# Mean layers: extra columns summed in a zeroed room of their own, among the additions of gathered quads, and added to the sums in seven wide parts

## The chip, the cores and the metric

The kernel runs on one core of a Trainium2 chip. The metric is the device time of one execution in microseconds (us), as the median of a few runs. Engines are named as in the profile: PE (TensorE matmul; PEld is its weight load), DVE (VectorE), ACT (ScalarE), POOL (GpSimd), SP (SyncE, which here issues transfers). "L2227" is line 2227 of the kernel before.

## The reference, cut to what matters

The program is a chain of four graph networks on 6250 nodes of 128 features and 106250 edges sorted by destination. The change lies in the third of them, three mean ("SAGE") layers in a row, and in the residual sum after them:

```python
deg = segment_sum(ones(src.shape[0]), dst, num_segments=n)
inv_deg = (1.0 / maximum(deg, 1.0))[:, None]
def sage_conv(h, Wl, b, Wr):
    agg = segment_sum(h[src], dst, num_segments=n) * inv_deg
    return agg @ Wl + b + h @ Wr
h = relu(sage_conv(x, W_l0, b0, W_r0))
h = relu(sage_conv(h, W_l1, b1, W_r1))
x = layernorm(x + sage_conv(h, W_l2, b2, W_r2))
```

## The kernel before, in words

Nodes lie in 49 blocks of 128 (`BLOCKS`), edges in 832 tiles of 128 (`TILES`). The sum over edges, `agg` (features on partitions, one column for each node), is made in two ways at once in each mean layer.

**Gathered tiles.** 288 tiles (`RUN`) are gathered. POOL issues one indirect DMA for a tile (L2140, `pool_rows`), 16 slots of `G` deep: before the first tile of quad q it waits until PE has used quad q-4. ACT makes one-hot matrices (L2148). PE multiplies a quad of four tiles into one of three banks (L2162, `pe_sum_quad`; 8 matmul records for each quad) and must find the additions of quad q-3 done. DVE adds each of the four 128x128 results to a window of `agg` whose start is read from a table (L2227): 72 quads, q = 0 to 71.

**Dense part.** All other edges are in an adjacency matrix in DRAM, which SP loads (L2102, L2107, `sp_adjacency`, four slots) and PE multiplies with three bf16 planes of the node rows (L2126, `pe_dense`) in 115 steps. Steps 0 to 16 give 544 "extra" columns (`extra`, one for each dense tile: what falls to the tile's first node). Steps 17 to 65 and 66 to 114 give the sums of two halves of the other nodes. `keep_extras` (L2210) copies the extras out of the banks, `add_half` (L2202) adds a half, five windows of 418 columns, to `agg`; PE waits for each (`adj_read`) before it uses the banks again. PE's order is written out by hand: behind step n come the quads `quads_by(n)` to `quads_by(n + 1)`, so that quads 0 to 3 come before step 17, about two quads follow three steps from there on, quads 36 and 37 come before step 66, and quad 71 comes last.

**Extras.** DVE adds each extra column to `agg` at a start read from the table: 8 after the additions of every quad from quad 4 (`EARLY_QUADS`) to quad 71 (`add_extras`, L2193). Each waits for the one before it.

After quad 71 come `add_half(1)` and one last addition of 418 columns (L2236). Then the next block of the program begins: PE multiplies `agg` with the weights (L2026). In the third mean layer, DVE also adds the residual, `hT += xT` over all 6272 columns (L2233), after quad 40; SP has loaded `xT` from DRAM (L2335) between the adjacency steps 40 and 41.

Of the kernel before, what the change touches and what calls it, by code (L numbers as in the profile page):

```python
# [15 lines left out]
P = 128  # L16
NODES = 6250
EDGES = 106250
D = 128
# [119 lines left out]
def build_program(nc, a, out):  # L139
    with ExitStack() as ctx:  # L140
# [130 lines left out]
        c_extra = signal("extra_added")  # L271
        residual_in = signal("residual_in")
        runs_ready = signal("runs_ready")
# [1891 lines left out]
        EXTRAS_A_QUAD = 8  # L2165
        EARLY_QUADS = quads_by(FIRST_STEPS)
        assert (RUN_QUADS - EARLY_QUADS) * EXTRAS_A_QUAD >= DENSE
        EXTRA_ADDS = DENSE + 2 * NODE_BANKS

        def dve_sums(l):  # L2170


            n = [0, 0]

            def after_adds():
                dve.wait_ge(c_added.sem, c_added.at(n[0]))

            def after_extra():
                if n[1]:
                    dve.wait_ge(c_extra.sem, c_extra.at(n[1]))  # L2180

            extras_left = [DENSE]
# [12 lines left out]

            def add_half(half):
                after_adds()
                dve.wait_ge(adj_used.sem, adj_used.at(FIRST_STEPS + (half + 1) * BLOCKS))
                for c in range(NODE_BANKS):
                    w = agg[:, bass.ds(chunk_start(DVE, half * NODE_BANKS + c), BANK_COLS)]  # L2200
                    after_extra()
                    dve.tensor_tensor(w, w, bank[c][:, 0:BANK_COLS], ALU.add).then_inc(c_extra.sem, 1)  # L2202
                    n[1] += 1
                after_extra()
                dve.sem_inc(adj_read.sem, 1)
# [7 lines left out]

            half_quads = quads_by(FIRST_STEPS + BLOCKS) - 2
            for q in range(RUN_QUADS):
                if q == EARLY_QUADS:
                    keep_extras()
                if q == half_quads:
                    add_half(0)
                windows = window_at(DVE, DENSE + q * QUAD, QUAD)  # L2220
                dve.wait_ge(c_rows.sem, c_rows.at(q + 1))
                after_extra()
                for k in range(QUAD):
                    if n[0]:
                        after_adds()
# [8 lines left out]
            add_half(1)  # L2234

            dve.tensor_tensor(agg[:, 0:BANK_COLS], agg[:, 0:BANK_COLS], agg[:, NODES:], ALU.add)  # L2236

        def sums_passed():
# [4 lines left out]
            for c, n in ((c_rows, RUN_QUADS), (c_onehot, RUN_QUADS), (c_far, RUN_QUADS), (c_added, RUN), (c_extra, EXTRA_ADDS), (adj_used, STEPS), (adj_read, 3),  # L2243
# [83 lines left out]
        for l in range(1, 3):  # L2327
            with nc.Block() as block:
                @block.sync
                def _(_e):  # L2330
                    sp_sage_weights(l)
                    sp_adjacency(0, FIRST_STEPS + BLOCKS // 2)
                    if l == 2:
                        sp.wait_ge(own_rows.sem, own_rows.at(GROUPS))
# [53 lines left out]
            if l == 2:  # L2388
                residual_in.passed(16)
# [387 lines left out]
```

## Time and profile before

| | |
|---|---|
| median of 3 runs | 7239.66 us (7233.92 to 7249.64) |
| the profiled execution's own time | 7241.22 us |
| its span | 7239.4 us |
| the three mean layers, from the first gather to the first matmul behind the last | about 4737 to 6028 us |
| busy share of the span | PE 76%, DVE 65%, ACT 31%, POOL 69% |

The rows below come from that execution. In a row of the timeline the first number is the start (us from the span's start), the second the length, then engine, line, operation, the tiles out<-in, the shape, and how many instructions were merged; in brackets is the idle time of the engine before them and what ended it.

### The profile page before, as it was taken

Reading aid. Unit: us, or ns where it says so; the run is one execution under the profiler, and the core shown is the slowest. Engines: PE = TensorE matmul, PEld = TensorE weight load, DVE = VectorE, ACT = ScalarE, POOL = GpSimd, SP = SyncE. Lnnn points to the kernel's source line nnn. Section 1 sums busy time; section 2 is a strip of 40 time slices with the busy share of each in tenths; the row PEclk is TensorE's granted clock in tenths of the full one; section 3 lists DMA queues with packets and bytes.
Section 4 is the critical chain, followed back from the end, with each engine's and each line's share of the span. In section 5 each row is a group of like instructions: output and inputs, shape, how many; then the busy total and the mean of one; then the engine's idle time right before and its main releaser. Section 6 shows DMA issues by size and latency. Waiting matters only on the chain. (4 is left out here: it accounts for less than half of the span.)

```text
span 7239.4 us, 119762 instructions
## 1 busy us (share of the span) xinstructions
PE 5528.3 (76%) x30345; PEld 4159.5 (57%) x30345; DVE 4732.1 (65%) x20294; ACT 2265.0 (31%) x5973; POOL 4967.1 (69%) x5179
## 2 busy tenths in 40 slices
PE   4675667777777767777767777789898996888887
PEld 3442344556656556656656566666665665666665
DVE  7985678466666456666546666664545556888887
ACT  1044443211114311113411112543333333454554
POOL 5777764677777577777577777657475673777774
PEclk7688888788888778888878888899999997998898
DMA  9433352577777467777567777667576762222222
GB/s 306 133 79 87 78 114 51 164 207 208 207 211 220 140 193 209 209 210 221 159 179 208 208 205 209 185 185 208 159 207 179 209 205 73 56 57 56 56 57 53
DMA packets 911701, 1151.31 MB, mean 159 GB/s; under 512 B 143234, under 2 KB 676290, under 8 KB 911106
## 3 DMA queue, kind: packets, MB, share of 16 engines
q1 hardware_dynamic: 689296, 673.54, 30.7%
q0 software_dynamic: 202464, 461.07, 23.8%
q10 hardware_dynamic: 19346, 9.66, 0.5%
q8 instruction: 265, 4.34, 0.2%
q14 instruction: 330, 2.70, 0.1%
HBM read 882.09 MB, written 261.74 MB: 158 GB/s over the span
## 5 line engine op out<-in xcount | busy, mean ns | idle before, releaser
L498 POOL DMA_INDIRECT G<-table_kv,idx x2496 | 2381.6, 954 | 956.0 <-issue 744.6
L1708 DVE SCALAR_TENSOR_TENSOR sums<-ramp,place,bank 128x128 f32<-128x128 f32 x2496 | 718.6, 343 | 1180.1 <-PE bank L1627 1084.3
L1617 PE MATMUL bank<-ident,G 128*128 128x128 f32 x2496 | 649.2, 337 | 708.0 <-DMA G<-table_kv,idx 701.1
L2140 POOL DMA_INDIRECT G<-table_h,src_idx x864 | 823.0, 953 | 480.5 <-issue 256.6
L1596 ACT COPY slab<-bank 128x512 f32<-128x512 f32 x624 | 364.0, 583 | 2293.4 <-PE bank L1617 2293.2
L498 POOL DMA_INDIRECT G<-table_h,idx x832 | 828.9, 996 | 301.4 <-issue 228.2
L1627 PE MATMUL bank<-qT,slab 128*128 x4992 | 906.9, 339 | 99.6 <-issue 82.2
L1617 PEld LDWEIGHTS bank<-ident,G 128*128 128x128 f32 x2496 | 382.7, 164 | 928.1 <-DMA G<-table_kv,idx 885.5
L1627 PEld LDWEIGHTS bank<-qT,slab 128*128 128x128 f32 x4992 | 793.9, 242 | 197.8 <-issue 196.8
L1839 DVE TENSOR_SCALAR OH<-ramp,place,weight 128x128 f32<-128x128 f32 x2076 | 721.7, 357 | 13.8 <-issue 6.9
L2126 PE MATMUL bank<-sums,qT 128*128 128x418 bf16 (+1 forms) x3528 | 672.2, 333 | 33.4 <-DVE same L2049 12.3
L1671 PE MATMUL bank<-OH,sums 128*128 128x128 f32 x3648 | 627.0, 327 | 24.2 <-DVE sums L1848 16.0
L898 POOL DMA_INDIRECT adjacency<-sums x544 | 526.9, 969 | 171.2 <-issue 165.2
L2602 PEld LDWEIGHTS bank<-OH,qT 128*128 128x128 f32 x3328 | 466.6, 223 | 283.0 <-DVE qT L2667 246.0
L2602 PE MATMUL bank<-OH,qT 128*128 128x128 f32 x3328 | 494.8, 311 | 127.2 <-DVE sums L2680 125.8
L1671 PEld LDWEIGHTS bank<-OH,sums 128*128 128x128 f32 x3648 | 564.0, 236 | 46.5 <-DVE sums L1848 28.3
L1848 DVE TENSOR_TENSOR sums<-sums,bank 128x128 f32 x1824 | 506.5, 278 | 3.6 <-issue 2.7
L2193 DVE TENSOR_TENSOR sums<-sums,rows 128x1 f32 x1632 | 267.0, 164 | 346.9 <-DVE sums L2227 108.3
L2126 PEld LDWEIGHTS bank<-sums,qT 128*128 128x128 bf16 x3528 | 346.0, 98 | 256.8 <-issue 36.2
L2148 ACT ACTIVATE OH<-ramp,place 128x128 f32<-128x128 f32 x864 | 275.9, 390 | 673.9 <-PE bank L2162 666.0
L2227 DVE TENSOR_TENSOR sums<-sums,bank 128x128 f32 x864 | 249.7, 289 | 213.3 <-DVE sums L2193 83.5
L2680 DVE TENSOR_TENSOR sums<-sums,bank 128x256 f32 x832 | 347.2, 417 | 62.3 <-issue 59.4
(351 smaller groups left out, 9582.8 us busy)
## 6 DMA issues: line engine op xcount, KB each, us to landing
stash<-G SPq DMA_DIRECT2D x312, 512.0 KB
sums<-stash SPq DMA_DIRECT2D x624, 256.0 KB
sums<-adjacency SPq DMA_DIRECT2D x294, 522.5 KB
adjacency<-same SPq DMA_DIRECT2D x49, 1184.0 KB
same<-adjacency SPq DMA_DIRECT2D x90, 522.5 KB
G<-table_kv,idx POOLq DMA_INDIRECT x2496
sums<-adjacency SPq DMA_DIRECT2D x48, 408.0 KB
table_kv<-G SPq DMA_DIRECT2D x72, 256.0 KB, 3.3
```

Of the source, the lines that this page charges most:

```text
L498: pool.indirect_dma_start(G[:, s, 0:width], None, tab, bass.IndirectOffsetOnAxis(ap=idx[:, s:s + 1], axis=0)).then_inc(c_gather[s].sem, 16)
L898: pool.indirect_dma_start(adj_cells, bass.IndirectOffsetOnAxis(ap=cell[:, d:d + 1], axis=0), count[:, d:d + 1], None).then_inc(scattered[i ...
L1596: act.copy(quad(KT, q).rearrange("p s d -> p (s d)"), bank[q % 2][:, :]).then_inc(c_kt.sem, 1)
L1617: ins = pe.transpose(bank[q % 2][:, (s % QUAD) * P:(s % QUAD + 1) * P], G[:, s, 0:D], ident[:])
L1627: ins = pe.matmul(bank[2 + q % 2][:, (s % QUAD) * P:(s % QUAD + 1) * P], KT[:, s, :], w, start=True, stop=True)
L1671: ins = pe.matmul(into[:, k * P:(k + 1) * P], v_rows[:, s, :], OH[:, s, :], start=True, stop=True)
L1708: ins = dve.scalar_tensor_tensor(scratch[:, s, :], ramp[:], place[:, n * QUAD + s:n * QUAD + s + 1], bank[2 + q % 2][:, s * P:(s + 1) * P] ...
L1839: ins = dve.tensor_scalar(OH[:, s, :], ramp[:], place[:, t:t + 1], weight[:, t:t + 1], ALU.is_equal, ALU.mult)
L1848: dve.tensor_tensor(w, w, bank[SUM_BANKS[q_add % 2]][:, k * P:(k + 1) * P], ALU.add).then_inc(c_added.sem, 1)
L2126: ins = pe.matmul(bank[c][:, 0:width], plane[k][:, b * P:(b + 1) * P], adj_slot[s][:, j * at + c * width:j * at + (c + 1) * width], start= ...
L2140: pool.indirect_dma_start(G[:, s, 0:D], None, table[l], bass.IndirectOffsetOnAxis(ap=src_idx[:, DENSE + t:DENSE + t + 1], axis=0)).then_in ...
L2602: ins = pe.matmul(o, msg[:, s, part * D:(part + 1) * D], OH[:, s, :], start=True, stop=True)
```

## The change

Four things. The `xT` space, which holds nothing that is needed in this stage, is zeroed in seven parts before quad 0. The extra columns are added there, at their node's column, and no longer to `agg`: 10 in a quad, in the quads 4 to 58, two or three ahead of each of the quad's four additions. After the quads 59 to 65, one part of 896 columns of `xT` is added to `agg`. And since `xT` is taken, the residual of the third layer goes through other spaces in four pieces (16, 16, 1 and 16 blocks): three are loaded before adjacency step 17, the fourth before step 41 once the first has been added, and they are added to `hT` after the quads 12, 16, 17 and 34. Each chain of additions waits for its own predecessor: an extra for the extra before it, an addition to `agg` for the addition to `agg` before it.

```diff
-        EXTRAS_A_QUAD = 8
+        EXTRAS_A_QUAD = 10
         EARLY_QUADS = quads_by(FIRST_STEPS)
+        EXTRA_QUADS = -(-DENSE // EXTRAS_A_QUAD)
+        PLACED_QUAD = EARLY_QUADS + EXTRA_QUADS
+        PLACED_PARTS = 7
+        PLACED = NP // PLACED_PARTS
+        RESIDUAL_QUADS = (EARLY_QUADS + 8, EARLY_QUADS + 12, EARLY_QUADS + 13, EARLY_QUADS + 30)
+        FIRST_RESIDUALS = 3
...
-            def add_extras(k):
-                after_adds()
-                done = DENSE - extras_left[0]
-                extras_left[0] -= k
-                for d in range(done, done + k, QUAD):
-                    windows = window_at(DVE, d, QUAD)
-                    for j in range(QUAD):
-                        after_extra()
-                        w = agg[:, bass.ds(windows[j], 1)]
-                        dve.tensor_tensor(w, w, extra[:, d + j:d + j + 1], ALU.add).then_inc(c_extra.sem, 1)
-                        n[1] += 1
...
+            def place_extra(d, node):
+
+                dve.wait_ge(c_extra.sem, c_extra.at(X_PARTS + d))
+                w = xT[:, bass.ds(node, 1)]
+                dve.tensor_tensor(w, w, extra[:, d:d + 1], ALU.add).then_inc(c_extra.sem, 1)
+
+            for part in range(X_PARTS):
+                dve.memset(xT[:, part * PLACED:(part + 1) * PLACED], 0.0).then_inc(c_extra.sem, 1)
             half_quads = quads_by(FIRST_STEPS + BLOCKS) - 2
             for q in range(RUN_QUADS):
                 if q == EARLY_QUADS:
                     keep_extras()
                 if q == half_quads:
                     add_half(0)
+                done = max(0, q - EARLY_QUADS) * EXTRAS_A_QUAD
+                extras = range(done, min(DENSE, done + EXTRAS_A_QUAD) if q >= EARLY_QUADS else done)
                 windows = window_at(DVE, DENSE + q * QUAD, QUAD)
-                dve.wait_ge(c_rows.sem, c_rows.at(q + 1))
-                after_extra()
+                places = dict(zip(extras, window_at(DVE, done, len(extras)) if extras else ()))
                 for k in range(QUAD):
-                    if n[0]:
-                        after_adds()
+                    for d in extras[len(extras) * k // QUAD:len(extras) * (k + 1) // QUAD]:
+                        place_extra(d, places[d])
+                    if k == 0:
+                        dve.wait_ge(c_rows.sem, c_rows.at(q + 1))
+                    after_last()
                     w = agg[:, bass.ds(windows[k], P)]
                     dve.tensor_tensor(w, w, bank[SUM_BANKS[q % 3]][:, k * P:(k + 1) * P], ALU.add).then_inc(c_added.sem, 1)
-                    n[0] += 1
-                if q >= EARLY_QUADS and extras_left[0]:
-                    add_extras(min(EXTRAS_A_QUAD, extras_left[0]))
-                if l == 2 and q == half_quads + 4:
-                    dve.wait_ge(residual_in.sem, residual_in.at(16))
-                    dve.tensor_tensor(hT[:], hT[:], xT[:], ALU.add)
+                    next_is(c_added, q * QUAD + k + 1)
+                part = q - PLACED_QUAD
+                if part in range(PLACED_PARTS):
+                    if part == 0:
+                        dve.wait_ge(c_extra.sem, c_extra.at(X_PARTS + DENSE))
+                    at = slice(part * PLACED, (part + 1) * PLACED)
+                    add_whole(agg[:, at], xT[:, at])
+                if l == 2 and q in RESIDUAL_QUADS:
+                    r = RESIDUAL_QUADS.index(q)
+                    dve.wait_ge(residual_in.sem, residual_in.at(16 * max(r + 1, FIRST_RESIDUALS)))
+                    home, b0, nb = residual_rows(r)
+                    dve.tensor_tensor(nodes_h[:, b0:b0 + nb, :], nodes_h[:, b0:b0 + nb, :], home, ALU.add).then_inc(residual_added.sem, 1)
             add_half(1)
...
+        def residual_rows(r):
+
+            b0 = (0, SLAB_BLOCKS, BLOCKS - 1, 2 * SLAB_BLOCKS)[r]
+            slab_rows = slab[:, 0:SLAB_BLOCKS * D].rearrange("p (b d) -> p b d", d=D)
+            home = (slab_rows, G[:, :, D:2 * D], dst_part[:, 0:D].unsqueeze(1), slab_rows)[r]
+            return home, b0, home.shape[1]
...
                     sp_sage_weights(l)
-                    sp_adjacency(0, FIRST_STEPS + BLOCKS // 2)
+                    sp_adjacency(0, FIRST_STEPS)
                     if l == 2:
-                        sp.wait_ge(own_rows.sem, own_rows.at(GROUPS))
-                        sp.dma_start(xT[:].rearrange("p (b d) -> p b d", d=D), table[0].rearrange("(b p) d -> p b d", p=P)).then_inc(residual_in.sem, 16)
+                        for r in range(FIRST_RESIDUALS):
+                            sp_residual(r)
+                    sp_adjacency(FIRST_STEPS, FIRST_STEPS + BLOCKS // 2)
+                    if l == 2:
+                        sp.wait_ge(residual_added.sem, residual_added.at(1))
+                        sp_residual(FIRST_RESIDUALS)
                     sp_adjacency(FIRST_STEPS + BLOCKS // 2, STEPS)
```

## Rows read from the trace of the kernel before

**Rows 1.** Waits by engine pair, PE only, 5149 to 5588 and 5588 to 6028.

```profile
PE bank L2026 <- PEq L2251: 22.1, 1, 22.1
PE bank L2026 <- PEq L2328: 21.5, 1, 21.5
...
PE bank L2026 <- PEq L2328: 21.8, 1, 21.8
PE bank L2126 <- DMA sums<-adjacency: 4.2, 1, 4.2
```

**Rows 2.** Timeline of PE and DVE, end of layer one; last row: layer two.

```profile
5126.06 1.13 PE L2162 MATMUL bank<-OH,G 128*128 128x128 f32 x8
...
5139.57 1.55 DVE L2227 TENSOR_TENSOR sums<-sums,bank 128x128 f32 x4 [0.45 <-DVE sums L2193]
5141.65 1.03 DVE L2193 TENSOR_TENSOR sums<-sums,rows 128x1 f32 x4 [0.53 <-DVE sums L2227]
5143.03 1.03 DVE L2193 TENSOR_TENSOR sums<-sums,rows 128x1 f32 x4 [0.35 <-DVE sums L2193]
5144.48 3.48 DVE L2202 TENSOR_TENSOR sums<-sums,bank 128x418 f32 x5 [0.41 <-DVE sums L2193]
5148.10 0.60 DVE L2236 TENSOR_TENSOR sums<-sums 128x418 f32<-128x418 f32 x1
...
5560.88 1.13 PE L2162 MATMUL bank<-OH,G 128*128 128x128 f32 x8 [0.42 <-issue]
```

**Rows 3.** Gathers L2140 by stretch: us, POOL busy (count), PEclk, DMA share, GB/s.

```profile
4785.40:5124.80 339.40, 256.66 (x272) 0.99 0.70 208
5219.30:5558.70 339.40, 256.65 (x272) 0.99 0.70 208
5652.90:5998.20 345.30, 262.63 (x272) 0.99 0.72 214
```

**Rows 4.** By stretch: us; PE, PEld, DVE, ACT, POOL busy; PEclk, DMA share, GB/s.

```profile
4963.30:5127.20 163.90, 163.81 (x1007) 104.81 (x1007) 80.41 (x391) 57.22 (x150) 122.13 (x130) 0.99 0.69 200
5835.60:6006.00 170.40, 165.66 (x1007) 103.73 (x1007) 86.87 (x392) 57.22 (x150) 124.46 (x126) 0.99 0.65 191
...
5646.00:5656.00 10.00, 10.00 (x90) 9.30 (x90) 4.86 (x12) 3.23 (x10) 2.46 (x3) 1.00 0.28 81
```

**Rows 5.** Timeline: POOL gathers beside DVE additions of two SBUF operands.

```profile
5860.84 6.69 DVE L2233 TENSOR_TENSOR hT<-hT,xT 128x6272 f32<-128x6272 f32 x1
5861.40 6.95 POOL L2140 DMA_INDIRECT G<-table_h,src_idx  x1 [0.31 <-issue]
...
5170.70 0.68 DVE L2046 TENSOR_TENSOR sums<-hT,qT 128x512 f32<-128x512 f32 x1
5171.17 1.02 POOL L2140 DMA_INDIRECT G<-table_h,src_idx  x1 [0.30 <-issue]
5171.30 0.69 DVE L2047 TENSOR_TENSOR qT<-hT,qT 128x512 bf16<-128x512 f32 x1
```

**Rows 6.** Timeline: DVE in quads 0 to 3, PE at step 17.

```profile
5215.91 0.89 DVE L2081 TENSOR_TENSOR hT<-bank,bias_rows 128x512 f32<-128x512 f32 x2 [0.20 <-PE bank L2072]
5219.23 1.55 DVE L2227 TENSOR_TENSOR sums<-sums,bank 128x128 f32 x4 [2.43 <-PE bank L2162]
5221.08 1.55 DVE L2227 TENSOR_TENSOR sums<-sums,bank 128x128 f32 x4 [0.30 <-DVE sums L2227]
5226.12 1.55 DVE L2227 TENSOR_TENSOR sums<-sums,bank 128x128 f32 x4 [1.45 <-PE bank L2162]
...
4794.64 1.94 PE L2126 MATMUL bank<-sums,qT 128*128 128x418 bf16 x10 [1.83 <-DVE rows L2210]
5662.08 1.94 PE L2126 MATMUL bank<-sums,qT 128*128 128x418 bf16 x10 [1.83 <-DVE rows L2210]
```

**Rows 7.** A memset of DVE: ns minimum/median/maximum.

```profile
L1948 DVE MEMSET rows<- x3: 698/698/698, 1320.3 to 3592.1; 128x768 f32 x3
```

**Rows 8.** The residual's transfer L2335, from issue to landing (minimum, median, maximum).

```profile
DMA to landing us min/median/max: 18.1/18.1/18.1
```

More of the change, by code:

```diff
@@ L271, in build_program @@
         c_extra = signal("extra_added")
+        c_whole = signal("whole_parts_added")
         residual_in = signal("residual_in")
+        residual_added = signal("residual_added")
         runs_ready = signal("runs_ready")
@@ new lines, in build_program, with after_last, next_is, add_whole @@
+        PLACED_QUAD = EARLY_QUADS + EXTRA_QUADS
+        PLACED_PARTS = 7
+        PLACED = NP // PLACED_PARTS
+        assert PLACED_QUAD + PLACED_PARTS <= RUN_QUADS and PLACED * PLACED_PARTS == NP
+        RESIDUAL_QUADS = (EARLY_QUADS + 8, EARLY_QUADS + 12, EARLY_QUADS + 13, EARLY_QUADS + 30)
+        FIRST_RESIDUALS = 3
+        WHOLE_ADDS = PLACED_PARTS + 2 * NODE_BANKS
+        def dve_sums(l):
+            last = []
+            def after_last():
+                for sem, n in last:
+                    dve.wait_ge(sem, n)
+            def next_is(c, n):
+                last[:] = [(c.sem, c.at(n))]
+            wholes = [0]
+            def add_whole(w, part):
+                after_last()
+                dve.tensor_tensor(w, w, part, ALU.add).then_inc(c_whole.sem, 1)
+                wholes[0] += 1
+                next_is(c_whole, wholes[0])
@@ L2196, in add_half @@
             def add_half(half):
-                after_adds()
                 dve.wait_ge(adj_used.sem, adj_used.at(FIRST_STEPS + (half + 1) * BLOCKS))
                 for c in range(NODE_BANKS):
-                    w = agg[:, bass.ds(chunk_start(DVE, half * NODE_BANKS + c), BANK_COLS)]
-                    after_extra()
-                    dve.tensor_tensor(w, w, bank[c][:, 0:BANK_COLS], ALU.add).then_inc(c_extra.sem, 1)
-                    n[1] += 1
-                after_extra()
+                    add_whole(agg[:, bass.ds(chunk_start(DVE, half * NODE_BANKS + c), BANK_COLS)], bank[c][:, 0:BANK_COLS])
@@ L2205, in add_half @@
+                after_last()
                 dve.sem_inc(adj_read.sem, 1)
@@ L2238, in sums_passed, with sp_residual @@
+        assert SLAB_BLOCKS == SLOTS and 3 * SLAB_BLOCKS + 1 == BLOCKS
+        def sp_residual(r):
+            home, b0, nb = residual_rows(r)
+            sp.dma_start(home, table[0][b0 * P:(b0 + nb) * P, :].rearrange("(b p) d -> p b d", p=P)).then_inc(residual_in.sem, 16)
         def sums_passed():
@@ L2242, in sums_passed @@
                 c.passed(16 * len(range(k, STEPS, ADJ_SLOTS)))
-            for c, n in ((c_rows, RUN_QUADS), (c_onehot, RUN_QUADS), (c_far, RUN_QUADS), (c_added, RUN), (c_extra, EXTRA_ADDS), (adj_used, STEPS), (adj_read, 3),
+            for c, n in ((c_rows, RUN_QUADS), (c_onehot, RUN_QUADS), (c_far, RUN_QUADS), (c_added, RUN), (c_extra, X_PARTS + DENSE), (c_whole, WHOLE_ADDS), (adj_used, STEPS), (adj_read, 3),
                          (turned_rows, GROUPS), (turned_kept, GROUPS), (own_rows, GROUPS), (own_kept, GROUPS), (planes_ready, GROUPS), (residual_done, GROUPS),
@@ L2388, in build_program @@
             if l == 2:
-                residual_in.passed(16)
+                residual_in.passed(16 * (FIRST_RESIDUALS + 1))
+                residual_added.passed(FIRST_RESIDUALS + 1)
         wup = wts[:, 0:D]
```

14 lines of the change are left out of this document (3 added, 11 removed).

## The prediction

> **What bounds the kernel now.** I read the waits of PE over the mean layers first. PE's longest waits are three of 21.5 to 22.1 us, one behind each mean layer [rows 1]. The timeline shows what PE waits for: its last quad ends at 5127.19, and DVE goes on to 5148.70, adding quads 69 to 71, their extras, the second half and the last 418 columns, before the next block starts at 5149.30 [rows 2, 1]. DVE is some 2.5 quads behind by then, because one of its quads with 8 extras takes about 4.95 us (0.45 + 1.55 + 0.53 + 1.03 + 0.35 + 1.03) [rows 2], against 163.9/34 = 4.82 us of PE (34 quads and 49 steps in the second half) [rows 4].
>
> Before that tail it is not DVE that sets the pace. POOL's 272 gathers of quads 4 to 71 take 339.4 us in the first two layers, 1.248 us each and without a pause [rows 3], that is 4.99 us for a quad, and PE's last quad ends 2.4 us after the last gather is issued (5124.8, 5127.19) [rows 3, 2]. So in the first layer POOL's chain and PE's end together; in the second PE ends at 5562.0, 3.3 us after POOL [rows 2, 3], which leaves POOL about 0.9 us of slack. In the third POOL takes 345.3 us [rows 3] and PE's second half 170.4 us instead of 163.9 [rows 4]: DVE's residual addition of 6.69 us holds up a gather (6.95 us instead of 0.94) [rows 5] and puts DVE so far behind that PE must wait for banks.
>
> **The change part by part.**
>
> *Extras leave the tail.* They end with quad 58, the parts with quad 65, so quads 66 to 71 are additions only: 1.85 us from one to the next (5219.23, 5221.08) [rows 6], and DVE will wait for PE. The new gap of PE behind a layer is 0.14 (a quad's end to its first addition, my estimate from waits between engines) + 1.55 + 0.41 + 3.48 + 0.14 + 0.60 + 0.60 to the next block = 6.9 us [rows 2]. Against 22.1, 21.5 and 21.8 [rows 1] this saves 15.2 + 14.6 + 14.9 = **44.7 us**. It holds whenever DVE is caught up by quad 71.
>
> *A quad with ten extras.* Chained extras follow at (1.03 - 0.16)/3 = 0.29 us [rows 2]. The trace does not show one between additions. Where an operation waits for nothing recent, it can start about when the one before ends: L2047 starts at 5171.30, before L2046's recorded end at 5171.38 [rows 5]. So I count 6 chained steps x 0.29, 4 from extra to addition x 0.16, 3 from addition to extra x 0.29, and the last addition with two table loads behind it, 0.29 + about 0.7 (one load leaves 0.30 to 0.45 idle [rows 6, 2]): 4.2 us. Upper bound: each of the 14 at its chained pitch, 4 x 0.42 + 10 x 0.29 + 0.7 = 5.3 us. I take 4.2, as nothing recent is waited for. Below 4.82 it costs nothing: PE's matmuls cover it.
>
> *Seven wide parts.* From 418 columns in 0.60 and 6272 in 6.69 us [rows 2, 5] a column costs 1.04 ns, so 896 take 1.09 us. With two chained waits a quad takes 3.1 us, under PE's 4.82, so nothing on DVE. But both operands lie in SBUF, as with L2233, and then a gather that starts during the addition is held until it ends: the gather of 5861.40 ended 0.86 after L2233, that of 5171.17 was 0.08 longer because L2046 ran until 5171.38 [rows 5]. With a gather every 1.248 us an addition of length L under that costs POOL L²/(2 x 1.248) on average, 0.48 us for a part, **3.3 us** a layer (bounds: 0, and 7 x 1.09 = 7.6). The Trainium skill, "SBUF — State Buffer", section "Who interferes with whom", says that a DVE instruction with two SBUF inputs contends with a GpSimd instruction that reads SBUF, but infers that `tensor_tensor` leaves descriptor generation alone; by the inference the 3.3 would be 0. The 6.95 us gather [rows 5] speaks against the inference, and that case is a rival below.
>
> *The residual in four pieces.* 16 blocks are 2048 columns, 6.69 - 4224 x 0.00104 = 2.29 us. Longer than the gathers' period, each costs POOL 2.29 - 0.62 = 1.67, three of them 5.0 us (bounds 0 and 6.9), against the 6.0 (6.95 - 0.94) of before. On DVE they come one at a time, while there is time to spare.
>
> *The memsets.* 0.698 us for 768 columns [rows 7] make 0.81 for 896, 5.7 in all. In the second layer DVE is free from 5216.80, so quad 0 is added at about 5222.5 instead of 5219.23; the idle times before quads 2 and 3 take up part, quad 3 comes at 5222.5 + 3 x 1.85 = 5228.05 instead of 5226.12, and PE's step 17 about 2 us late [rows 6]. In the first layer DVE is free earlier before quad 0, and nothing that PE waits for is late. The 2 us cost nothing on the end: POOL's chain starts with PE's quad 0, which is not moved, and a later PE waits less for gathers. If that cover were gone, it would be 2 us in each of two layers.
>
> *Transfers.* Issuing and landing 33 of 49 blocks early takes at most 18.1 x 33/49 = 12.2 us [rows 8], from about 5646 to 5658, when the DMA engines are 28% busy [rows 4]; step 17 is needed at 5662 to 5664 [rows 6]. They are queued ahead of the loads of steps 17 to 20 on SP, each next needed 2.7 us or more apart, so I take 0. The 16 blocks before step 41 are 5.9 us; the 18.1 us of before cost a PE wait of 4.2 [rows 1], so anything under 14 us is hidden.
>
> **The sum.** PE ends its layer when POOL's chain lets it. First layer: +3.3. Second: 3.3 less 0.9 of slack and rounding, +2.3. Third: POOL ends at 5998.2 - 6.0 + 5.0 + 3.3 = 6000.5, PE 2.4 later at 6002.9 instead of 6006.0, -3.1. (PE alone would end there at about 5664 + 332.6 = 5996.7, the 332.6 being the first layer's time from step 17 on, 4794.64 to 5127.19 [rows 6, 2].) Together +2.5. With the tails -44.7 + 2.5 = **-42.2 us**. The profiled execution took 7241.2 (span 7239.4), so 7199.0; the median of the runs is 1.6 lower, so **7197.5 us**. 0.2% is 14.5 us, about what a measurement of this kernel can tell from no change.
>
> **Rivals.**
> 1. *The wide additions do not hold gathers*, the Trainium skill's inference. Then layer one ends where it did, layer two gains 0.4, layer three ends with PE's own 5996.7, -9.3: -44.7 - 9.7 = -54.4, **7185**. Against it stands the 6.95 us gather [rows 5]; for it, no gather lengthened by the single-column extras, which have two SBUF operands as well. Chance 0.12.
> 2. *Every wide addition catches a gather at its start*: +7.6, +6.6 and 5998.2 + 0.9 + 7.6 + 2.4 = 6009.1, +3.1: -27.4, **7212**. Or transfers and clock eat as much. Chance 0.09.
> 3. *Interleaving hides nothing*: a quad takes 5.3 us. PE may be held once DVE is some 12 us behind (two to three quads, three banks). 55 quads take PE 55 x 4.82 + 4 at the half = 269, so PE loses 55 x 5.3 - 281 = 10.5 us in the first two layers and some 7 in the third, in place of the +2.5: about -17, **7222**. The Trainium skill, "VectorE: DVE Perf Modes", section "The DRAIN you can't avoid", says that the next DVE operation starts only when the pipe is empty, semaphore or not; by that each step would cost its chained pitch. The 5171.30 start before 5171.38 [rows 5] speaks against it. Chance 0.06.
> 4. *The other side: DVE's instruction handling, not its data, is the limit*, 14 operations with table starts each 0.1 us dearer, and the two loads on top: 5.7 us a quad. It decides from 5.38 us, where 55 x 5.38 - 281 = 15 equals the tail saved. At 5.7 PE loses 32.5 a layer: 3 x (32.5 - 14.9) = +53, **7290**. For it: every such operation has its own address step; against: 12 operations with such steps fit into 4.95 us now, chained, three loads included. Chance 0.03.
>
> The forecast has 0.70, and its own range is 7188 to 7208. The range that leaves out 2 in 10 or less takes rivals 1 and 2 in: 7183 to 7218. Faster by over 0.2% are the forecast, rivals 1 and 2 and most of 3: 0.95; within 0.2% 0.02; slower 0.03.
>
> **What would show it.** PE's gap behind each mean layer near 7 us; L2202's second group about 2 us behind PE's last quad; quads 4 to 58 at under 4.8 us on DVE when it does not wait; a few gathers of 1.1 to 2.0 us in quads 59 to 65, three of up to 3.2 in the third layer; POOL's 272 gathers at about 343 us in the first two layers and 348 in the third; no PE wait for `adjacency` there. A PE gap still over 12 us, or PE's second halves over 170 us, would make the prediction wrong.

## The result, and the profile after

The kernel after takes 7226.26 us (median of 12 runs, 7219.04 to 7230.33) against 7240.41 us (12 runs, 7233.92 to 7249.64) for the kernel before: ratio 0.998, interval 0.9971 to 0.9988. It is 14 us faster where 42 were forecast, and lies above the range of 7183 to 7218. The profiled execution took 7222.3 us (span 7220.5).

The mean layers alone, from the start of PE's quad 0 to the first matmul of the next block, went from 1106.7 to 1092.8 us, which is the same 14 us. For each layer, with PE's time from quad 0 to the end of quad 71 (times in us, read from the starts and lengths of PE's records):

| layer | PE quads 0 to 71, before | after | gap behind it, before | after | POOL's 272 gathers, after |
|---|---|---|---|---|---|
| 1 | 343.0 | 354.7 | 22.1 | 7.1 | 344.2 |
| 2 | 344.0 | 359.1 | 21.5 | 6.4 | 348.5 |
| 3 | 354.4 | 359.1 | 21.8 | 6.4 | 348.4 |

So the gaps gave 45.5 us back (forecast 44.7), and PE's own stretch lost 11.7 + 15.1 + 4.7 = 31.5 us (forecast 2.5). The whole miss is in the second number.

Lines of the kernel after: L2142 gathers, L2164 PE's quads, L2128 its dense steps, L2236 the additions of a quad, L2215 the extras, L2193 halves and wide parts, L2218 memsets, L2207 `keep_extras`, L2248 the residual, L2251 the last addition, L2028 the next block, L763 a load of starts from the table.

The tail of layer one, from the timeline of PE and DVE, beside [rows 2]:

```profile
5141.43 1.05 PE L2164 MATMUL bank<-OH,G 128*128 128x128 f32 x8
5142.61 1.55 DVE L2236 TENSOR_TENSOR sums<-sums,bank 128x128 f32 x4 [2.01 <-PE bank L2164]
5144.36 2.03 DVE L2193 TENSOR_TENSOR sums<-sums,bank 128x418 f32 x3 [0.20 <-DVE sums L2236]
5146.88 1.31 DVE L2193 TENSOR_TENSOR sums<-sums,bank 128x418 f32 x2 [0.48 <-DVE sums L2193]
...
5149.53 2.68 PE L2028 MATMUL bank<-wts,sums 128*128 128x128 f32 x11 [7.05 <-PEq L2281]
```

DVE waits 2.01 us for quad 71, so it is caught up, and nothing but additions stands between PE's last quad and the next block. PE's waits over the mean layers (us in total, times, longest), 4740 to 6019, and below them the same three kinds in the kernel before, 4740 to 6027:

```profile
PE bank L2164 <- issue: 24.6, 32, 2.1
PE bank L2128 <- DVEq L2202: 19.5, 3, 7.2
PE bank L2028 <- PEq L2358: 12.8, 2, 6.4
...
PE bank L2128 <- DVE rows L2207: 11.0, 3, 4.5
PE bank L2028 <- PEq L2281: 7.1, 1, 7.1
```

```profile
PE bank L2126 <- DVEq L2205: 11.3, 3, 4.1
...
PE bank L2126 <- DVE rows L2210: 5.5, 3, 1.8
PE bank L2162 <- issue: 5.0, 7, 1.5
```

The three gaps are now 7.1 + 12.8. The wait for `adjacency` of [rows 1] is gone. But at the half (`adj_read`, L2202) PE waits 19.5 us in three, where before it waited 11.3, and for the extras' copy (L2207) 11.0 instead of 5.5. Ahead of its quads (L2164) it stands for 24.6 us in 32 times instead of 5.0 in 7. The profile names no releaser there, but a quad must find the additions of the quad three before it done. All three say that DVE is late. Two consecutive quads of DVE, timeline (the number in brackets is DVE's idle time before the row):

```profile
4998.35 0.29 DVE L2236 TENSOR_TENSOR sums<-sums,bank 128x128 f32 x1
5001.19 0.45 DVE L2215 TENSOR_TENSOR xT<-xT,rows 128x1 f32 x2 [2.55 <-issue]
5001.68 0.29 DVE L2236 TENSOR_TENSOR sums<-sums,bank 128x128 f32 x1
5001.88 0.73 DVE L2215 TENSOR_TENSOR xT<-xT,rows 128x1 f32 x3
...
5004.12 0.29 DVE L2236 TENSOR_TENSOR sums<-sums,bank 128x128 f32 x1
5005.75 0.45 DVE L2215 TENSOR_TENSOR xT<-xT,rows 128x1 f32 x2 [1.34 <-issue]
...
5011.84 0.45 DVE L2215 TENSOR_TENSOR xT<-xT,rows 128x1 f32 x2 [2.55 <-issue]
```

The additions themselves run faster than forecast: an extra follows an addition at 0.20 us (5001.68 to 5001.88), an addition an extra at 0.13 in three cases of four and at 0.20 in the others. What is new is the idle time ahead of each quad, 2.55 and 1.34 us in turn. In it DVE's sequencer loads starts from the table. The loads of starts by line, first in the kernel after (one stretch of the first half), then before; the numbers are ns, minimum, median and maximum:

```profile
L763 DVEq TENSOR_LOAD <-start x63: 341/364/2314, 4795.5 to 4958.2; - x63
```

```profile
L761 DVEq TENSOR_LOAD <-start x95: 339/343/359, 4800.1 to 4957.7; - x95
```

Before, every load took 0.34 us. After, the quad's own four starts still take 0.34 us, and the load of ten extras' starts takes 2.30 us in one quad (at 4998.75) and 1.07 to 1.09 us in the next (at 5004.53). Without waits for PE a quad, from its first addition to the next quad's first, so takes 5.77 and 4.55 us in turn (5001.68 to 5006.25 is 4.57, 5006.25 to 5012.34 is 6.09 with a further wait of 0.3), 5.16 in the mean, against 4.93 of before and PE's 4.82. From the last addition of quad 4 to that of quad 58 DVE takes 286.1 us in layer one; before it took 275.9. PE's quad 58 starts 277.6 us after its quad 4, before 268.0.

PE's second half (from dense step 66 to quad 71) takes 169.7, 169.5 and 169.4 us, before 163.9, 164.8 and 170.3. So only 9.6 of the 31.5 us were lost there; the rest lies ahead of it, in the wait at the half and in the first half.

Step 17 of the second layer, timeline and granted clock (last two rows: stretch; length, busy PE, PEld, DVE, ACT, POOL; PEclk, DMA share, GB/s), beside [rows 6]:

```profile
5217.87 6.45 DVE L2218 MEMSET xT<- 128x896 f32 x7
5224.24 1.48 DVE L2236 TENSOR_TENSOR sums<-sums,bank 128x128 f32 x4
...
5229.71 1.55 DVE L2236 TENSOR_TENSOR sums<-sums,bank 128x128 f32 x4 [0.29 <-DVE sums L2236]
5231.17 0.78 DVE L2207 COPY rows<-bank 128x272 f32<-128x272 f32 x2
```

```profile
5232.10 3.64 PE L2128 MATMUL bank<-sums,qT 128*128 128x418 bf16 x10 [4.45 <-DVE rows L2207]
5235.53 1.86 PE L2128 MATMUL bank<-sums,same 128*128 128x418 bf16 x5
```

```profile
5232.10:5236.90 4.80, 4.80 (x14) 2.06 (x15) 0.32 (x2) 0.00 (x0) 3.58 (x5) 0.50 0.19 49
5238.00:5242.00 4.00, 4.00 (x28) 2.73 (x27) 2.07 (x12) 2.02 (x6) 3.08 (x4) 1.00 0.71 190
```

The seven memsets take 6.45 us (each 0.805, one every 0.94), quad 3 is added 3.6 us later than before, PE waits 4.45 instead of 1.83 us, and behind that wait its clock is granted at 0.50 (1.2 of 2.4 GHz), so the step itself takes 3.64 and 1.86 us instead of 1.94 and 1.05. From quad 0 to quad 4 that is 18.26 us instead of 13.14.

The wide parts and the gathers beside them, layer two, and POOL's 272 gathers by stretch, beside [rows 3, 5]:

```profile
5531.51 1.09 DVE L2193 TENSOR_TENSOR sums<-sums,xT 128x896 f32<-128x896 f32 x1
5546.89 1.09 DVE L2193 TENSOR_TENSOR sums<-sums,xT 128x896 f32<-128x896 f32 x1
```

```profile
5532.09 1.33 POOL L2142 DMA_INDIRECT G<-table_h,src_idx  x1 [1.54 <-PE bank L2164]
5547.03 1.77 POOL L2142 DMA_INDIRECT G<-table_h,src_idx  x1 [0.30 <-issue]
```

```profile
4789.07:5133.31 344.24, 259.01 (x272) 0.99 0.69 205
5220.30:5568.78 348.48, 258.82 (x272) 0.98 0.68 203
5654.12:6002.55 348.43, 262.59 (x272) 0.98 0.70 208
```

Each of these gathers ends 0.82 us after the addition beside it (5533.42 and 5532.60; 5548.80 and 5547.98), as the one beside L2233 ended 0.86 after it [rows 5]: it is held. But POOL is busy only 259.0 us in layer one, 2.4 more than before, while the stretch is 4.8 us longer, and the gather at 5532.09 waits 1.54 us for PE, for a slot of `G`. So PE, and no longer POOL, sets the end. In the third layer the pieces of the residual add theirs:

```profile
L2248 DVE TENSOR_TENSOR hT<-hT,slab x2: 2282/2282/2283, 5716.7 to 5832.6; 128x2048 f32<-128x2048 f32 x2
```

```profile
5717.82 1.97 POOL L2142 DMA_INDIRECT G<-table_h,src_idx  x1 [0.30 <-issue]
```

### The profile page after: what moved, and what is told of

Its sections match the earlier page's. It is cut to its first block and busy times, and to the rows that moved or that the text cites. A ratio compares the mean times of both kernels' runs of the same rounds, so it can differ in the third digit from the quotient of the medians.

```text
span 7220.5 us, 119527 instructions
## 1 busy us (share of the span) xinstructions
PE 5533.5 (77%) x30306; PEld 4172.2 (58%) x30345; DVE 4709.3 (65%) x20339; ACT 2265.6 (31%) x5973; POOL 4969.2 (69%) x5179
## 5 line engine op out<-in xcount | busy, mean ns | idle before, releaser
L2142 POOL DMA_INDIRECT G<-table_h,src_idx x864 | 827.9, 958 | 477.4 <-issue 256.0
L1629 PEld LDWEIGHTS bank<-qT,slab 128*128 128x128 f32 x4992 | 808.9, 246 | 196.5 <-issue 195.8
L2128 PE MATMUL bank<-sums,qT 128*128 128x418 bf16 (+1 forms) x3528 | 675.7, 334 | 42.4 <-DVEq L2202 19.5
L2215 DVE TENSOR_TENSOR xT<-xT,rows 128x1 f32 x1632 | 260.1, 159 | 448.2 <-issue 315.1
L1850 DVE TENSOR_TENSOR sums<-sums,bank 128x128 f32 x1824 | 501.4, 275 | 3.2 <-issue 2.1
L2128 PEld LDWEIGHTS bank<-sums,qT 128*128 128x128 bf16 x3528 | 347.3, 99 | 267.4 <-issue 52.9
L2150 ACT ACTIVATE OH<-ramp,place 128x128 f32<-128x128 f32 x864 | 275.9, 390 | 708.4 <-PE bank L2164 687.6
L881 POOL DMA_INDIRECT G<-table_gated,src_idx x288 | 283.9, 986 | 150.3 <-issue 84.7
L2715 DVE TENSOR_TENSOR sums<-sums,bank 128x256 f32 x832 | 343.7, 413 | 61.7 <-issue 58.4
```

The source lines that it names most:

```text
L1629: ins = pe.matmul(bank[2 + q % 2][:, (s % QUAD) * P:(s % QUAD + 1) * P], KT[:, s, :], w, start=True, stop=True)
L1850: dve.tensor_tensor(w, w, bank[SUM_BANKS[q_add % 2]][:, k * P:(k + 1) * P], ALU.add).then_inc(c_added.sem, 1)
L2128: ins = pe.matmul(bank[c][:, 0:width], plane[k][:, b * P:(b + 1) * P], adj_slot[s][:, j * at + c * width:j * at + (c + 1) * width], start= ...
L2142: pool.indirect_dma_start(G[:, s, 0:D], None, table[l], bass.IndirectOffsetOnAxis(ap=src_idx[:, DENSE + t:DENSE + t + 1], axis=0)).then_in ...
```

## The experiments

The runs fell on chips of two kinds. On two of them (and in the runs above) the kernel before takes 7239 to 7256 us, on three others 9600 to 9721 us. Every run was compared with the kernel before on its own chip, and each says which kind it had. The changed kernels without a ratio ran once. The first nine, on the slower kind, could not answer for the time, and show only durations.

**One load of ten, or loads of at most four (slower kind; the kernel before 9605.21 us there).** The first kernel loads the ten starts in 4, 4 and 2; the second is the kernel before with one load of eight.

```diff
-                places = dict(zip(extras, window_at(DVE, done, len(extras)) if extras else ()))
+                places = dict(zip(extras, [v for at in range(done, done + len(extras), QUAD) for v in window_at(DVE, at, min(QUAD, done + len(extras) - at))]))
```

```diff
-                for d in range(done, done + k, QUAD):
-                    windows = window_at(DVE, d, QUAD)
-                    for j in range(QUAD):
+                for d in range(done, done + k, 2 * QUAD):
+                    windows = window_at(DVE, d, 2 * QUAD)
+                    for j in range(2 * QUAD):
```

> The changed kernel, with one edit: the ten table starts of a quad's extras are read by loads of 4, 4 and 2 values instead of one load of 10. Theory A (the load of 10 values, 1.07 or 2.30 us against 0.34 for 4, makes DVE's quad 5.2 us and so holds PE): three loads of about 0.38 replace a mean of 1.69, a quad falls to about 4.6 us, under PE's 4.82, PE is no longer held in quads 25 to 58, and the whole is about 32 us faster than the changed kernel, near 7194. Rival B (what holds PE is the interleaved additions themselves, or gathers held by the wide parts): the loads were covered or the cost is per value, a quad stays at 5.1 to 5.2 us and the time within 5 us of 7226.

> The kernel before, with one edit: the eight starts of a quad's extras come by one load of 8 values instead of two loads of 4. Theory A, cost by width: the load takes 1.07 us or more, a DVE quad 5.4 instead of 4.95, and each mean layer grows by 20 us and more, in all about 7300 or above. Theory A', cost by where the row of ten starts (40-byte steps, not 16-byte ones): the load takes 0.35 to 0.45 us, a quad falls to 4.6, and the time is 10 to 20 us below 7240. Rival B expects the latter as well.

The first took 9570.4 us (ratio 0.9965, interval 0.9942 to 0.9988). Its DVE quads take 6.00 and 4.76 us, more than with the one load, and not the 4.6 that I had expected. Its timeline, the last addition of one quad and the first extras of the next, twice:

```profile
6901.37 0.45 DVE L2215 TENSOR_TENSOR xT<-xT,rows 128x1 f32 x2 [2.79 <-issue]
...
6906.13 0.45 DVE L2215 TENSOR_TENSOR xT<-xT,rows 128x1 f32 x2 [1.54 <-issue]
```

In one quad its three loads take 0.35, 0.34 and 0.53 us, in the next 0.97, 0.97 and 0.52. The same four values cost 0.34 or 0.97, and the quads differ only in where their first value lies: at a multiple of four values (of 16 bytes) in the cheap ones, two values behind one in the dear ones. With the load of ten (1.07 and 2.30) and the load of eight of the second kernel (0.595, at multiples of eight) all durations follow from about 0.25 us for each four values that start at a multiple of 16 bytes, about 0.22 for each other value, and 0.1 besides; a load that starts elsewhere counts single values throughout. This rule is fitted to these durations; for a load of twelve it gives 0.85 us, and 0.85 was measured later. So my theory then, that the number of values alone was at fault, fell: the start counts for most. The second kernel took 9608.46 us, its quad still 4.96 us: one load of 0.595 took the place of two of 0.34, between the two outcomes that I had expected.

**A ladder of loads.** 

> The changed kernel with 25 more table loads behind the first mean layer's sums, of 1 to 16 values from different starts; nothing uses them. Theory A: the duration steps up between 4 and 10 values whatever the start, to 1.07 us and 2.30 us at widths to be found. Theory A': loads of 8, 12 and 16 values from starts that are multiples of 4 take 0.4 us, those from starts 2, 10 and 30 over 1 us. The time grows by the sum of these loads, 10 to 40 us.

Twenty-five loads of other sizes and starts, put ahead of the mean layers, left no instruction in the trace, probably since nothing used their values. The run is a second one of the kernel after (9627.15 us), and the sizes stayed unmeasured apart from those above.

**The extras ahead of the additions, not among them (slower kind, beside the first kernel).**

```diff
-                    for d in extras[len(extras) * k // QUAD:len(extras) * (k + 1) // QUAD]:
+                    for d in extras if k == 0 else ():
```

> As e1_split4, but all ten extras of a quad stand ahead of its first addition instead of two or three ahead of each. Where an operation that waits for nothing recent starts early (what the forecast counted on): a quad takes 10 x 0.29 + 4 x 0.42 + about 1.3 for loads, some 5.9 us instead of 4.6, PE is held for about 40 us in each layer and the time is near 7300. Where a DVE operation always starts only when the pipe is empty: the same time as e1_split4 within 5 us.

With the same loads of 4, 4 and 2, a quad takes 7.13 and 5.90 us, 6.52 in the mean against 5.38 with the extras among the additions, and the run 9640.92 us. The timeline of one quad:

```profile
6906.42 1.90 DVE L2215 TENSOR_TENSOR xT<-xT,rows 128x1 f32 x7 [1.94 <-issue]
6908.66 0.74 DVE L2215 TENSOR_TENSOR xT<-xT,rows 128x1 f32 x3 [0.34 <-DVE xT L2215]
6909.45 1.55 DVE L2236 TENSOR_TENSOR sums<-sums,bank 128x128 f32 x4
```

Ten chained extras take 2.98 us, four chained additions 1.55. Interleaving saves 1.13 us a quad. The cause of rival 3 is refuted by this and by the pitches of 0.20 and 0.13 us.

**Loads of twelve and eight in turn.** Quads with twelve and with eight extras alternate, so that every load starts at a multiple of 16 bytes. The second kernel also moves the memsets behind `keep_extras`, the third is the kernel before with the change's residual alone.

```diff
-                done = max(0, q - EARLY_QUADS) * EXTRAS_A_QUAD
-                extras = range(done, min(DENSE, done + EXTRAS_A_QUAD) if q >= EARLY_QUADS else done)
+                odd = max(0, q - EARLY_QUADS) % 2
+                done = max(0, q - EARLY_QUADS) * EXTRAS_A_QUAD + 2 * odd
+                extras = range(done, max(done, min(DENSE, done + (8 if odd else 12))) if q >= EARLY_QUADS else done)
```

```diff
-            for part in range(X_PARTS):
-                dve.memset(xT[:, part * PLACED:(part + 1) * PLACED], 0.0).then_inc(c_extra.sem, 1)
             half_quads = quads_by(FIRST_STEPS + BLOCKS) - 2
...
                 if q == EARLY_QUADS:
                     keep_extras()
+                    for part in range(X_PARTS):
+                        dve.memset(xT[:, part * PLACED:(part + 1) * PLACED], 0.0).then_inc(c_extra.sem, 1)
```

> The changed kernel again, for the runs beside it on the same chip. On a chip on which the kernel before takes 7240 us: 7226, DVE's loads of ten starts at 1.07 and 2.30 us in turn. On one on which PE is slower (the kernel before at 9600): the ratio is lower than 0.998, since DVE's 5.2 us quads no longer hold PE there.

> The changed kernel with 12 and 8 extras in turn, in place of 10 in each quad, so that every load begins at a multiple of four starts and is of whole fours. Theory A (a load costs about 0.25 us for each aligned four and 0.22 us for each single value besides, a misaligned one being all singles): loads of 0.85 and 0.60 us in turn, mean 0.72 instead of 1.69, a DVE quad at about 4.3 us instead of 5.2, PE no longer held in quads 25 to 58; where the kernel before takes 7240 us, 7226 less some 25 to 32. Rival B (the interleaved additions or held gathers hold PE): a quad stays over 5 us and the time within 5 us of the changed kernel's.

> As e5_alt12_8, and the seven memsets stand behind the copy of the extras (ahead of quad 4) instead of ahead of quad 0. If the memsets make step 17 late in the second and third layer (18.2 us from quad 0 to quad 4 instead of 13.1): that falls back to 13.1, and the time is 0 to 8 us under e5's, the less the more gathers set the end of a layer. If not: no difference.

> The kernel before with one part of the change alone: the residual in four pieces through other spaces. By the forecast's term: gathers are held for 3.3 to 5.0 us instead of 6.0, no PE wait for the adjacency load at quad 20, DVE not pushed back by 6.7 us at once; the third layer from quad 0 to the last quad 4 to 10 us shorter than before (354.4 us there), the others unchanged. Rival: DVE's lag alone sets it, less than 2 us.

> The kernel of e6_alt_late_zero again, to see it where PE is as quick as in the profile of before. Theory A: if the kernel before takes about 7240 us here, this takes 7185 to 7200, a DVE quad takes 4.3 us when it does not wait, and no PE wait for banks is left. If the kernel before takes 9600 to 9700 here, as in the runs before, PE is slower than DVE anyway and the time is within 20 us of e6's.

All fell on the slower kind (the kernel before 9721.01 us; for the last 9605.97). The kernel after took 9681.36 (0.9969, 0.9947 to 0.9992), the alternating one 9692.8 (0.9977, 0.9959 to 0.9995), with late memsets 9693.88 (0.9972, 0.9956 to 0.9988), the residual alone 9735.95. With late memsets again, on another chip, it was 9573.27, where the kernel before takes 9605.97. I had expected it within 20 us of the first such run; that failed, and only the ratio to the kernel before is alike. The first three differ by less than their runs scatter, although DVE's quad fell from 5.16 to 4.21 us (4.37 and 4.04 in turn). The reason is PE: on that kind of chip it takes some 5.9 us for a quad, and stops with no wait that the profile shows. PE's waits there in most of a layer (6700 to 7120), from the split kernel, and one stretch of it by engine:

```profile
PE bank L2128 <- issue: 36.9, 51, 3.3
```

```profile
6700.00:6860.00 160.00, 140.43 (x817) 85.84 (x817) 64.43 (x376) 51.28 (x135) 101.95 (x109) 0.97 0.54 176
```

On the quicker kind PE is busy 163.81 of 163.90 us [rows 4], and in the first half of layer one (4801 to 4955) 151.9 of 154.0 us. A DVE that needs 5.16 us a quad is covered by such a PE, and so is one that needs 4.21. The gaps behind the layers are 6.4 to 7.1 there too; with the extras in the tail (the kernel before with a load of eight, and the residual alone) they are 13.7 to 15.3.

**Making DVE the bound on that kind of chip.** The first kernel makes the load of ten twice and uses values of both. The next three leave out the third plane in the dense steps 17 to 114 and every second gather, of the kernel after, of the alternating one, and of the kernel before, so that PE and POOL are faster than DVE. (The kernel before 9600.17 us there.) The last is the alternating one of these with late memsets, which fell on the quicker kind (the kernel before 7256.03 us).

```diff
-                places = dict(zip(extras, window_at(DVE, done, len(extras)) if extras else ()))
+                loads = [window_at(DVE, done, len(extras)) for _ in range(2)] if extras else []
+                places = {d: loads[i % 2][i] for i, d in enumerate(extras)}
```

```diff
-                for k in range(3):
+                planes = 3 if n < FIRST_STEPS else 2
+                for k in range(planes):
...
+                if t % 2:
+                    continue
                 pool.indirect_dma_start(G[:, s, 0:D], None, table[l],
```

> The changed kernel, and each quad's ten starts are loaded twice (half of the extras use the one copy, half the other): the suspected cost doubled, nothing else. Theory A: a DVE quad takes 5.16 + 1.7 = 6.9 us; on this chip PE needs some 5.9 us for a quad, so PE is held for about 55 x 6.9 - (55 x 5.9 + 12) = 43 us a layer: 465 us from quad 0 to the last quad instead of 422. Rival B (interleaving or held gathers): the loads are hidden, 422.

> The changed kernel with PE and POOL lightened, so that PE is quicker than DVE, as on the chip of the profile: it leaves out the third plane in dense steps 17 to 114 and every second gather. PE alone would need about 4.4 us a quad here. Theory A: DVE's 5.16 us set the pace of the quads 4 to 58, PE waits for banks there, lag 12 us.

> x2_light_after with 12 and 8 extras in turn, loaded from starts that are multiples of four (e5's edit). Theory A: a DVE quad takes 4.21 us, so PE sets the pace and each layer ends 25 to 35 us sooner than in x2, in all 75 to 105 us. Rival B: within 5 us of x2.

> The kernel before with the same two things left out as in x2: DVE's 4.93 us a quad set the pace to quad 71, and the tail is 22 us. From quad 0 to the next block: x2 differs from it by -15 for the tail and +13 for 55 quads that are 0.23 us longer, less 13 quads that are shorter, in all -10 to -30 us a layer; x3 is 40 us and more a layer under it.

> x3_light_alt (third plane and every second gather left out), with the seven memsets behind the copy of the extras. If the memsets ahead of quad 0 make the copy and step 17 late in the second and third layer: the time from quad 0 to quad 4 falls there by 1 to 4 us from 16.6 and 17.4, and the copy comes about 2.5 us sooner behind PE's quad 3; quad 4's own additions may come later by up to 2 us. If they don't: 16.6 to 17.4 again.

The doubled load took 9734.45 us, PE's stretch 466.2, 462.0 and 463.4 us, as expected (465). Its timeline, two quads:

```profile
6906.06 0.45 DVE L2215 TENSOR_TENSOR xT<-xT,rows 128x1 f32 x2 [4.89 <-issue]
...
6911.74 0.49 DVE L2215 TENSOR_TENSOR xT<-xT,rows 128x1 f32 x2 [2.45 <-issue]
```

The idle times grow from 2.55 and 1.34 to 4.89 and 2.45: by the 2.30 and 1.07 of the added loads. A load is paid for in full on DVE, and above PE's pace on PE's end.

| less work on PE and POOL | us | DVE's quad | PE quads 0 to 71, three layers |
|---|---|---|---|
| kernel before | 9388.21 | 4.93 | 344.7, 345.9, 350.0 |
| kernel after | 9336.96 | 5.78 and 4.55 | 344.9, 345.4, 344.0 |
| alternating | 9169.42 | 4.37 and 4.04 | 290.3, 291.9, 296.0 |
| alternating, late memsets (quicker kind) | 7039.66 | 4.37 and 4.04 | 291.2, 290.9, 294.9 |

Where DVE is the bound, the alternating loads save 167.5 us, in one run each. I had expected 75 to 105. The part that is due to DVE's pace is 55 x (5.16 - 4.21) = 52 us for each layer, 157 for three, and the stages became 156 us shorter (1053.9 to 897.8): I had expected PE to hold the kernel at some point above DVE's pace, and it did not. The other 11 us lie outside these stages, within what single runs of that kind differ by. The kernel before, at 4.93 us a quad, needs as long as the kernel after in layers one and two: what the latter loses at 5.16 us up to quad 58 it gains in the shorter quads behind.

For the last kernel I had expected 1 to 4 us less from quad 0 to quad 4 in layers two and three, where 16.6 and 17.4 us had been measured. It is 12.3 us in all three layers. But layer one, where the memsets hardly delay step 17 (13.3 us in the kernel after, 13.1 in the kernel before), fell as well (15.2 to 12.3), so about 3 us of this belong to the kind of chip.

**The same on a quicker chip (the kernel before 7239.35 us, 7227.38 to 7245.85, 13 runs).** The four kernels are the kernel after, the alternating one, the alternating one with late memsets, and the residual alone.

> The changed kernel, beside the next ones. On a chip on which the kernel before takes 7240 to 7256 us: ratio 0.998, PE's last quads 354 to 359 us behind quad 0 in each layer, as in its first profile.

> e5's kernel (12 and 8 extras in turn, loads of whole fours) on a chip where PE is quick. Theory A: DVE's quads take 4.21 us, PE is no longer held, from quad 0 to the last quad 343 to 350 us in the first layer and up to 352 in the others, and the whole is 25 to 32 us faster than f1, near 0.994 of before. Rival B: within 5 us of f1.

> e6's kernel: f2 with the memsets behind the copy of the extras. From quad 0 to quad 4 13.1 us instead of 18.2 in the second and third layer; the time 0 to 8 us under f2's, less where the gathers set a layer's end.

> e7's kernel (the kernel before, with the residual in four pieces alone) where PE is quick: the third layer from quad 0 to the last quad 4 to 10 us shorter than the 354.4 of before, the other two as before.

| kernel | us (runs) | ratio, interval | PE quads 0 to 71 | stages |
|---|---|---|---|---|
| after | 7223.04 (10) | 0.9979, 0.9969 to 0.9988 | 354.5, 359.4, 358.6 | 1092.4 |
| alternating | 7194.24 (4) | 0.9938, 0.9921 to 0.9954 | 348.0, 343.7, 348.6 | 1060.1 |
| alternating, late memsets | 7191.35 (4) | 0.9937, 0.992 to 0.9953 | 345.3, 344.1, 346.5 | 1055.8 |
| residual alone | 7229.23 (1) | | 343.0, 343.3, 347.9 | 1099.4 |

The alternating loads alone save 28.8 us, and bring the change to 45 us below the kernel before, where 42 were forecast. PE's 24.6 us ahead of its quads are gone from its waits, and those at the half are 9.8 us in three instead of 19.5. Its loads, two of its quads, and PE at the half in layer one:

```profile
L763 DVEq TENSOR_LOAD <-start x48: 343/350/855, 4958.6 to 5067.6; - x48
```

```profile
5001.22 0.29 DVE L2237 TENSOR_TENSOR sums<-sums,bank 128x128 f32 x1
5002.62 0.74 DVE L2215 TENSOR_TENSOR xT<-xT,rows 128x1 f32 x3 [1.11 <-issue]
...
5006.45 0.29 DVE L2237 TENSOR_TENSOR sums<-sums,bank 128x128 f32 x1
5007.60 0.45 DVE L2215 TENSOR_TENSOR xT<-xT,rows 128x1 f32 x2 [0.86 <-issue]
```

```profile
4958.62 1.94 PE L2128 MATMUL bank<-sums,qT 128*128 128x418 bf16 x10 [3.29 <-DVEq L2202]
```

No load takes over 0.86 us, the idle times are 1.11 and 0.86, and at the half PE waits 3.29 us and goes on at full clock. In the kernel after the same row is:

```profile
4972.76 3.64 PE L2128 MATMUL bank<-sums,qT 128*128 128x418 bf16 x10 [7.19 <-DVEq L2202]
```

POOL now sets the end: PE's last quad ends 2.1, 2.2 and 2.7 us after the last gather is issued. The gathers held by wide additions are then what is left:

```profile
4781.80:5126.34 344.54, 261.94 (x272) 1.00 0.65 205
5206.20:5546.35 340.15, 257.55 (x272) 0.99 0.67 208
5625.52:5970.00 344.48, 261.88 (x272) 0.99 0.68 211
```

Against the 339.4 of [rows 3], layer one loses 5.1 us in which seven gathers are held for 5.3 in all, layer two 0.8 with one held for 0.9. The late memsets take the first 18.2 and 18.4 us of layers two and three (quad 0 to quad 4) back to 13.1. The place of the memsets is the only difference there:

```profile
5208.20 1.94 PE L2128 MATMUL bank<-sums,qT 128*128 128x418 bf16 x10 [1.83 <-DVE rows L2207]
```

Yet layer two's PE stretch stays (343.7 and 344.1): behind POOL's chain the 5 us cost nothing. What the stages gained (4.3 us) is in layers one and three, where 3.1 and 1.3 us less are lost in held gathers. In time, 7191.35 against 7194.24 with ranges that overlap, it can't be told from no change. It is the best version measured, 48 us below the kernel before.

The residual in pieces alone takes 6.5 us off the third layer's stretch (354.4 to 347.9), by one profile each; its single time of 7229.23 us lies within the runs of the kernel before. PE's wait for `adjacency` is gone there too.

## Why the prediction was right and wrong

- **The tails: right.** 15.1 + 15.1 + 15.4 = 45.5 us were saved for 44.7 forecast, with gaps of 7.05, 6.40 and 6.41 for 6.9.
- **The step that failed: "a quad with ten extras", 4.2 us.** In it, "two table loads behind it" were put at about 0.7 us, from the idle times behind loads of four starts. One of the two became a load of ten, 1.07 or 2.30 us. The quad takes 5.16 us, nearly the "upper bound" of 5.3, but the bound was reached by the wrong term: the chained steps are shorter than I took them, the loads 0.6 to 1.9 us longer. 5.16 is over PE's 4.82, so DVE falls behind until PE is held for banks. The rule beside it, that a quad under 4.82 costs nothing, held: at 4.21 us PE's stretches are 348.0, 343.7 and 348.6 us.
- **The signs of being wrong did not show it.** The gaps are under 12 us and PE's second halves under 170 us, and still 31.5 us were lost. Of the signs named for the forecast, DVE's quad of under 4.8 us was the one that failed; POOL's 272 gathers took 344.2, 348.5 and 348.4 us, for about 343, 343 and 348.
- **Rival 3 had the place and the price of it, by another cause.** It gave 7222; 7226 was measured. That this is so near is in part luck, since the pace came from another term. Its sum at the pace that DVE really had (5.23 us a quad from quad 4 to 58, its waits included: (286.1 - 3.9)/54) is 55 x 5.23 - 281 = 6.7, and it had left out the first half on DVE, some 4 us: 10.7, against 11.7 measured in layer one. The Trainium skill, "VectorE: DVE Perf Modes", section "The DRAIN you can't avoid", has the next operation wait for the empty pipe, by which the interleaving would hide nothing; the same section adds that a next operation that is not held starts earlier. These traces agree with the addition: 0.20 and 0.13 us between unchained steps against 0.29 chained, and 5.38 against 6.52 us a quad. That PE pays for DVE's pace is shown three ways: the doubled load, the lighter kernels, and the alternating loads, which alone take the 29 us away again.
- **Rival 4's threshold, 5.38 us a quad, was nearly reached.** Its cause (each operation dearer) is not there.
- **The wide parts: right in kind, near in size.** A part takes 1.09 us, as forecast, and holds gathers. Held time is 2.4, 2.2 and 2.7 us in the layers of the kernel after, for 3.3 forecast; in the alternating kernel 5.3 and 0.9 in the first two. An average is fair, but one layer may be 3 us off it. Rival 1 is refuted: the Trainium skill, "SBUF — State Buffer", section "Who interferes with whom", infers that `tensor_tensor` does not touch descriptor generation, and the gathers of 1.77 and 1.97 us beside it differ. In the kernel after these gathers cost nothing, since PE ended the layer.
- **The residual: right in kind.** Pieces of 2.28 us for 2.29. The three hold gathers for 3.3 us in all (1.97, 2.07 and 2.06 instead of 0.94) for 5.0 forecast.
- **The memsets: the size was off, and so was the cover.** 6.45 us for 5.7, as one follows another only every 0.94 us. Step 17 was 5.1 us later from quad 0, not 2: 2.6 of wait and 2.5 of matmuls at half clock behind it, which the forecast had not. "They cost nothing on the end" holds where POOL sets the end (layer two of the alternating kernel), and seems to fail in the kernel after, where layer two's stretch is 4.4 us longer than layer one's. No run moved the memsets of the kernel after alone, so this share is not shown.
- **The transfers: right.** No wait for `adjacency`.

What made the range too narrow is that the unknown was bounded on its chained steps alone. The load of ten values had no row in the trace of before, and it was given the price of a load of four without a bound above. The trace of before has loads of a single value (L767, 0.30 to 0.33 us); ten of them would have bounded it at some 3 us. At the 0.22 us for each further value, which only these runs show, it is 2.3.

## What to carry to other kernels

Loads from a table into an engine's registers belong in the sum of an engine's work, like its operations: change how many values one takes or where it starts, and its price is unknown until measured. Start them at multiples of 16 bytes, even if the work then comes in unequal portions (12 and 8 in place of 10 and 10). And when an engine near the bound gets more work per round, ask for each item that the trace has no row for what it costs at worst, whether or not it counts as busy in the profile.

## What the runs showed of the hardware

- A load of several 4-byte values into DVE's registers took 0.34 us for four, 0.60 for eight, 0.85 for twelve and 1.07 for ten values from a start at a multiple of 16 bytes, and 0.97 for four and 2.30 for ten from a start 8 bytes behind one. DVE does nothing meanwhile: a load added to each quad lengthened its idle time from 2.55 and 1.34 to 4.89 and 2.45 us.
- Where a chain of small additions waits for its own predecessor, a 128x1 addition follows the last after 0.29 us; between additions of another chain the steps are 0.13 to 0.20 us apart.
- Seven memsets of 0.805 us with nothing to wait for followed one another every 0.94 us.
- The same program takes 7240 us on some chips and 9600 to 9720 us on others. There, PE was busy 140.4 of 160 us in a stretch like one where it is busy 151.9 of 154.0 us on the first kind. The granted clock was 0.97 against 1.00, DMA moved 176 GB/s against 214, and the profile shows no releaser for PE's pauses. What causes them stays open.
- Behind gaps of PE of 4.45 and 7.19 us the clock was granted at 0.50 (5232.10 to 5236.90 and 4972.76 to 4977.80 in the kernel after), and ten matmuls took 3.64 us. Behind gaps of 1.83 and 3.29 us they took 1.94 us, and behind one of 3.86 us, in the kernel before, 3.29 us at a granted clock of 0.56 (4963.31 to 4966.50).
